# Chunk 0's turned keys and queries earlier on TensorE, one copy moved to ScalarE, and the first late sum of squares and the late root drawn forward

## The chip, the cores and the metric

One core of one Trainium2 chip runs the whole program. The metric is device time in microseconds (us) of one execution; the runs of the kernel before stand under the profile heading.

## The reference

Two transformer-like layers over x of shape (2, 1024, 128), all float32, in one launch:

```
xn = layernorm(x)
x  = x + attn(xn) + moe64(xn)      # layer 0
xn = layernorm(x)
x  = x + rwkv(xn) + moe8(xn)       # layer 1

attn:  h = layernorm(xn)*w + b; q,k,v = h @ qkv_w.T + qkv_b   (16 heads of 8)
       q = q/|q|, k = k/|k|; softmax(q @ k.T * sqrt(8)) @ v; xn + out @ out_w.T + out_b
moe64: top 3 of 64 experts, capacity 64; gelu(xe @ w1 + b1) @ w2 + b2, weighted sum
```

The change lies in the start of `attn`: q and k are divided by their lengths, written as pairs of float16 (a high and a low half), and turned so that the head dimension lies on the partitions.

## The kernel before

The 2048 tokens are 16 tiles of 128, worked in four chunks of 512 tokens (`NC` = 4, `CH` = 4). Chunks 0 and 1 (`EARLY` = 2) are the first sequence of 1024 tokens and are all that the attention needs at first; chunks 2 and 3 are prepared later, between the tiles of the attention.

A program is written by hand for each engine, and each engine runs its own list in the order written; semaphores join the lists. Nothing is scheduled by a planner, so a wait on one engine holds everything that stands behind it there.

The start of the program, chunk by chunk: TensorE turns the normalised rows, multiplies by the q, k and v weights and the gate (`queries_keys`, `value_rows`, `gate_logits`); VectorE adds the bias and stores q and k (`projected`, L724 and L728); ScalarE squares (L487), VectorE sums the squares per head (L715), ScalarE takes the root (L492), VectorE inverts it and scales k (L754 to L758), GpSimd scales q (L362); ScalarE writes the high halves (`high_keys` L497, `high_queries` L502), VectorE and GpSimd the low halves (`low_keys` L764, L367). TensorE then turns the halves with 16 transposes for each of keys and queries of a chunk into PSUM (the tensor `scores`, of four banks: keys in banks 0 and 1, queries in 2 and 3), and VectorE copies 2048 float16 of each partition to `KT` or `QT` (L734). The queries of chunk 1 are turned later, after tile 0 of the attention, into two other banks (`next_queries`, L1307 on TensorE, L748 on VectorE).

For chunks 2 and 3 GpSimd squares q and k (`late_squares`, L357), VectorE sums them (`late_sums`, L770), and ScalarE takes one root for both (L544, it waits for both sums). Directly behind that root ScalarE has the exponential of the decay (L546, which needs another table, loaded by ACT_TABLE_LOAD), and then all the exponentials of the attention (L558).

TensorE's list between the projections and the attention is: four transposes of the layer-1 weights and one of `small_rows` (L1277, L1279), turned keys 0, turned queries 0, turned keys 1 (L1295), and then, after waiting for `kt_sb` 2, `qt_sb` 1 and `lg_sb` 4, the scores. A tile of the attention is 128 keys by 512 queries by 4 heads: TensorE computes scores for two heads at a time (L1334, into `scores`), ScalarE takes the exponential of two banks (L558, two per tile), TensorE multiplies by the values (L1348). There are 128 tiles. Work of the 64-expert layer stands between the tiles at fixed tile numbers: the counts at tile 9, slots and late splits on VectorE at tiles 8 to 18, the inversion at 22, and six tiles for each of eight rounds of four pairs of experts from tile 32 on. The weight loads (L282, L286) are issued by SyncE when `late_split` and `inverted` have come. After the attention comes layer 1 (L1596, L1605, L1080).

VectorE, when keys 0 and 1 and queries 0 are copied, does the top 8 of the gate (L835, L838), the copy of chunk 1's queries (L748), and then the expert masks (L845 to L853).

Of the kernel before, what the change touches and what calls it, by code (L numbers as in the profile page):

```python
# [8 lines left out]
ACT = mybir.ActivationFunctionType  # L9
# [14 lines left out]
def build(nc, x_d, ln_w_d, ln_b_d, qkv_w_d, qkv_b_d, out_w_d, out_b_d, gate_w_d, gate_b_d, w1_d, b1_d, w2_d, b2_d,  # L24
# [4 lines left out]
    CH = 4  # L29
# [56 lines left out]
    with ExitStack() as ctx:  # L86
# [355 lines left out]
        def _(act):  # L442
# [55 lines left out]

            def high_queries(c):
                act.wait_ge(s["qn_ready"], c + 1)  # L500
                src = QKA[:, 0, CH * c:CH * c + CH, :].rearrange("p t (h d) -> p (t h) d", d=HD)
                a.activation(QSs[c][:, :, 0:2, :], src.unsqueeze(2).to_broadcast([P, CH * HEADS, 2, HD]), ACT.Copy).then_inc(s["hi_q"], 1)  # L502
# [39 lines left out]
            high_queries(1)  # L542
            act.wait_ge(s["late_sq"], NC - EARLY)
# [120 lines left out]
        def _(dve):  # L664
# [66 lines left out]
            def split_cols(c, dst, bank, ready, done):  # L731

                dve.wait_ge(s[ready], c + 1)
                v.tensor_copy(dst[:, :, BLK * c:BLK * c + BLK], S[:, bank:bank + 2].rearrange("p b n -> p (b n)").bitcast(F16)  # L734
                              .rearrange("p (g n) -> p g n", g=NHG)).then_inc(s[done], 1)

            def keys_cols(c):
                split_cols(c, KT, 0, "kt_ps", "kt_sb")

            def queries_cols(c):  # L740
                split_cols(c, QT, 2, "qt_ps", "qt_sb")
# [18 lines left out]
            def low_keys(c):  # L760
                dve.wait_ge(s["hi_k"], c + 1)
                k = KSs[c % 2]
                ka = QKA[:, 1, CH * c:CH * c + CH, :].rearrange("p t (h d) -> p (t h) d", d=HD)
                v.tensor_tensor(k[:, :, 1:4:2, :], ka.unsqueeze(2).to_broadcast([P, CH * HEADS, 2, HD]), k[:, :, 0:4:2, :],  # L764
                                ALU.subtract).then_inc(s["lo_k"], 1)

            def late_sums(c):

                dve.wait_ge(s["late_in"], c - EARLY + 1)
                v.tensor_reduce(NL[:, c - EARLY, :], TMPs[c % 2].rearrange("p (n d) -> p n d", d=HD), AX, ALU.add).then_inc(s["late_sq"], 1)  # L770
# [9 lines left out]
            projected(3)  # L780
            keys_cols(0)
            low_keys(1)
            queries_cols(0)
            late_sums(2)
            keys_cols(1)
            late_sums(3)
# [53 lines left out]
            next_queries()  # L840
# [6 lines left out]
            link(last)  # L847
            link(v.tensor_tensor(MH[:], EQ[:, 0], EQ[:, 1], ALU.add))
# [362 lines left out]
        def _(pe):  # L1211
# [60 lines left out]

            pe.wait_ge(s["w1_in"], 16 * 5)
# [7 lines left out]
            pe.wait_ge(s["const_ready"], 3)  # L1281
            pe.wait_ge(s["ht_sb"], NC)
            for c in range(EARLY):

                for src, bank, hi, lo, done, freed in ((KSs[c % 2], 0, "hi_k", "lo_k", "kt_ps", "kt_sb"),
                                                       (QSs[c % 2], 2, "hi_q", "lo_q", "qt_ps", "qt_sb"))[:2 - c]:
                    pe.wait_ge(s[hi], c + 1)
                    pe.wait_ge(s[lo], c + 1)
                    if c:
                        pe.wait_ge(s[freed], c)  # L1290
                    cols = src.rearrange("p (t g j) w d -> p t g (j w d)", t=CH, g=NHG)
                    for g in range(NHG):
                        dst = S[:, bank + g // 2].bitcast(F16).rearrange("p (g t n) -> p g t n", g=2, t=CH)
                        for t in range(CH):
                            last = tr(dst[:, g % 2, t, :], cols[:, t, g, :], ident16[:])  # L1295
                    last.then_inc(s[done], 1)
# [362 lines left out]
```

## Time and profile before

| what | value |
|---|---|
| median of 3 runs | 529.93 us (527.74 to 531.07) |
| the profiled execution: its time / span | 532.37 us / 530.6 us |
| PE (TensorE) busy | 488.2 us, 92% |
| ACT (ScalarE) busy | 373.5 us, 70% |
| DVE (VectorE) busy | 301.7 us, 57% |
| POOL (GpSimd) busy | 145.0 us, 27% |
| mean granted TensorE clock | 0.977 |

PE is TensorE's matmuls, ACT is ScalarE, DVE is VectorE, POOL is GpSimd. Times in the profile count from the start of the span. The busy shares are averages over stages with different limits; the change touches only the stretch from about 36 to 56 us, so what counts is who waits for whom there and what follows from the moment at which the exponentials begin.

### The profile page before, as it was taken

The numbers are of one execution on the slowest core, as the hardware profiler recorded it, in microseconds if no ns is written. First come the engines' busy times: TensorE is split into PE (matmuls) and PEld (weight loads), VectorE is DVE, ScalarE is ACT, GpSimd is POOL, SyncE is SP. The second block draws the span as 40 slices with busy tenths as digits, with TensorE's granted clock in tenths as the row PEclk, the third lists the DMA queues.
The fourth block names the chain that finished last, engine by engine and source line by source line (L and its number), as shares of the span: only waits on it lengthen the run. The fifth ranks groups of instructions, "written<-read, shape, count | busy, mean of one in ns | idle before, by whom it ended". The sixth has DMA issues, their size and how long they took to land.

```text
span 530.6 us, 11403 instructions
## 1 busy us (share of the span) xinstructions
PE 488.2 (92%) x4633; PEld 264.9 (50%) x4634; DVE 301.7 (57%) x791; ACT 373.5 (70%) x463; POOL 145.0 (27%) x133
## 2 busy tenths in 40 slices
PE   2974999999999999999998999999899999999996
PEld 1772323343464465464454232323366767776775
DVE  6689779734333533532521116158846993995895
ACT  3764888876889789878888999889734635543641
POOL 4069000110232032033000255515560647300120
PEclk9996799999999999999998999999999999999999
DMA  5200000193488787887641611100100020000000
GB/s 147 80 2 0 1 2 2 48 305 116 119 236 278 244 250 260 258 262 240 204 142 58 194 33 34 36 7 16 32 16 1 15 51 15 22 1 0 22 0 21
DMA packets 38542, 50.01 MB, mean 94 GB/s; under 512 B 3581, under 2 KB 20250, under 8 KB 38490
## 3 DMA queue, kind: packets, MB, share of 16 engines
q1 hardware_dynamic: 35524, 43.84, 25.5%
q0 software_dynamic: 2560, 5.25, 5.0%
q8 instruction: 37, 0.61, 0.5%
q10 hardware_dynamic: 406, 0.20, 0.1%
q14 instruction: 15, 0.12, 0.1%
HBM read 45.07 MB, written 4.19 MB: 93 GB/s over the span
## 4 chain that ended last, share of the span: by engine, by line
PE 49%; ACT 17%; DVE 6%; issue 5%; DVEq 0%
ACT region_b L558 11%; PE bank L1348 11%; PE bank L1605 9%; PE scores L1596 9%; PE scores L1334 5%; PE bank L1394 4%; PE bank L1382 3%; ACT xn L564 2%; PE bank L1404 2%; PE bank L1465 2%; DVE region_a L1069 2%; ACT L558 2%; ACT L564 2%; DVE base L1080 1%; PE bank L1359 1%
## 5 line engine op out<-in xcount | busy, mean ns | idle before, releaser
L558 ACT ACTIVATE region_b<-scores 128x1024 f32<-128x1024 f32 x256 | 242.4, 1046 | 51.6 <-PE scores L1334 51.4
L1348 PE MATMUL bank<-region_b 128*16 128x256 f32 x2048 | 149.2, 391 | 0.0
L1334 PE MATMUL scores<-region_b 32*128 32x512 f16 x512 | 83.5, 392 | 18.3 <-ACT region_b L558 15.8
L620 ACT ACTIVATE region_b<-scores,small_cols 128x512 f32<-128x512 f32 x64 | 43.5, 685 | 48.6 <-PE scores L1596 48.6
L388 POOL DMA_INDIRECT region_a<-xn_rows,slot_token x32 | 32.5, 1015 | 164.9 <-DVE h_rows L910 108.1
L1348 PEld LDWEIGHTS bank<-region_b 128*16 128x16 f32 x2048 | 42.0, 96 | 57.8 <-issue 42.4
L1605 PEld LDWEIGHTS bank<-region_a,region_b 128*128 128x128 f32 x512 | 62.0, 192 | 15.1 <-issue 15.0
L1334 PEld LDWEIGHTS scores<-region_b 32*128 32x128 f16 x512 | 20.9, 91 | 97.1 <-ACT region_b L558 71.3
L1605 PE MATMUL bank<-region_a,region_b 128*128 128x128 f32 x512 | 62.5, 276 | 0.0
L1596 PE MATMUL scores<-x_rows,region_a 128*128 128x512 f32 x128 | 60.8, 597 | 0.0
L1080 DVE SCALAR_TENSOR_TENSOR base<-bank,g,base 128x128 f32<-128x128 f32 x128 | 36.0, 343 | 25.8 <-PE bank L1605 25.5
L397 POOL DMA_INDIRECT xn<-slot_out,slot_gather x24 | 24.7, 1028 | 66.6 <-DMA slot_out<-slots_io 44.7
L910 DVE COPY h_rows<-bank 128x512 f32<-128x512 f32 x32 | 22.1, 692 | 24.6 <-PE bank L1382 24.6
L926 DVE TENSOR_TENSOR slots_io<-bank,region_a 128x512 f32<-128x512 f32 x8 | 5.5, 692 | 51.6 <-PE bank L1404 51.6
L1382 PE MATMUL bank<-region_a,slots_io 128*64 128x512 f32 x128 | 32.8, 610 | 0.2
L1404 PE MATMUL bank<-region_a,xn 128*64 128x128 f32 x512 | 32.4, 280 | 0.5 <-issue 0.5
L1404 PEld LDWEIGHTS bank<-region_a,xn 128*64 128x64 f32 x512 | 28.4, 139 | 7.8 <-issue 7.8
L1596 PEld LDWEIGHTS scores<-x_rows,region_a 128*128 128x128 f32 x128 | 22.3, 191 | 18.8 <-issue 18.6
L397 POOL DMA_INDIRECT y_rows<-slot_out,slot_gather x24 | 25.4, 1058 | 22.5 <-DMA y_rows<-slot_out,slot_gather 15.2
L817 DVE COPY av_out<-bank 128x512 f32<-128x512 f32 x16 | 11.1, 692 | 34.5 <-PE bank L1348 32.2
L918 DVE TENSOR_TENSOR xn<-bank,region_a 128x512 f32<-128x512 f32 x32 | 21.3, 687 | 15.6 <-PE bank L1394 15.6
L1394 PE MATMUL bank<-ident,h_rows 128*128 128x128 f32 x128 | 21.3, 299 | 0.0
(240 smaller groups left out, 559.8 us busy)
## 6 DMA issues: line engine op xcount, KB each, us to landing
region_a<-in_L_ffn_w SPq DMA_DIRECT2D x64, 512.0 KB, 5.5
region_a<-in_L_ffn_b SPq DMA_DIRECT2D x17, 128.0 KB, 7.0
slot_out<-slots_io SPq DMA_DIRECT2D x8, 256.0 KB, 7.6
region_a<-in_L_attn_x SPq DMA_DIRECT2D x4, 256.0 KB, 4.5
xn_rows<-xn SPq DMA_DIRECT2D x1, 1024.0 KB, 5.1
region_a<-in_L_ffn_W SPq DMA_DIRECT2D x1, 1024.0 KB, 6.3
out<-base SPq DMA_DIRECT2D x4, 256.0 KB, 2.3
region_a<-xn_rows,slot_token POOLq DMA_INDIRECT x32, 3.6
```

The costliest lines, as they stand in the source:

```text
L388: g.indirect_dma_start(ring_in[m % RING], None, xn_rows, bass.IndirectOffsetOnAxis(IDX[:, m:m + 1], 0), bounds_check=T - 1, oob_is_err=Tru ...
L397: g.indirect_dma_start(YGS[c % 2][:, t - CH * c, k, :], None, slot_out, bass.IndirectOffsetOnAxis(SLG[:, k, t:t + 1], 0), bounds_check=SLO ...
L558: a.activation(PR[:, n % PBUF, 2 * h:2 * h + 2, :], S[:, 2 * h:2 * h + 2, :], ACT.Exp, scale=SCALE).then_inc(s["exp_done"], 1)
L620: a.activation(HS[:, e % 2, k], ps[2 * (e % 2) + k][:], ACT.Relu, bias=COL[:, HC1 * e + k:HC1 * e + k + 1]).then_inc(s["relu_done"], 1)
L1080: last = v.scalar_tensor_tensor(y, ps[4 + 3 * (e % 2)][:, D * t:D * t + D], G8[:, c, t, e:e + 1], y, ALU.mult, ALU.add)
L1334: last = mm(S[:, j], KT[head, hg, keys], QT[head, hg, BLK * c:BLK * c + BLK], start=True, stop=True)
L1348: last = mm(AV[32 * j:32 * j + VW, cols], VA[:, tile, HG * (g % NHG) + j, :], PR[:, st % PBUF, j, cols], start=(st == 0 and half == 0), st ...
L1382: last = mm(ps[5 + i % 2][CAP * e:CAP * e + CAP, :], BT[:, P * i + CAP * e:P * i + CAP * e + CAP], ring_w1[i][:, e, :], start=True, stop=True)
L1394: last = tr(ps[5 + i % 2][:, P * c:P * c + P], cols[:, c, :], ident[:])
L1404: last = mm(ps[7][CAP * e:CAP * e + CAP, D * i:D * i + D], HTS[:, i, P * c + CAP * e:P * c + CAP * e + CAP], ring_w2[i][:, e, c, :], start ...
L1596: mm(ps[2 * (e % 2) + k][:], MW1[:, e, P * k:P * k + P], XN2T[:, c, :], start=True, stop=True).then_inc(s["up2"], 1)
L1605: last = mm(ps[4 + 3 * (e % 2)][:, D * t:D * t + D], HS[:, e % 2, k, P * t:P * t + P], MW2[:, e, k, :], start=(k == 0), stop=(k == HC1 - 1))
```

## The change

TensorE turns chunk 0's keys and queries directly behind the last gate logits, ahead of the layer-1 weights. Chunk 0's turned queries are copied by ScalarE (behind the high halves of chunk 1's queries, ahead of the late root) instead of VectorE. VectorE does the first long sum (chunk 2) and chunk 1's low key halves ahead of the copy of chunk 0's turned keys, and the second long sum ahead of the copy of chunk 1's turned keys. VectorE's copy of chunk 1's turned queries moves behind the three expert comparisons. Nothing is added or left out of the arithmetic.

```
 ScalarE
+            def queries_cols():
+                act.wait_ge(s["qt_ps"], 1)
+                a.activation(QT[:, :, 0:BLK], S[:, 2:4]...bitcast(F16)..., ACT.Copy).then_inc(s["qt_sb"], 1)
...
             high_queries(1)
+            queries_cols()
             act.wait_ge(s["late_sq"], NC - EARLY)
             a.activation(NL[:], NL[:], ACT.Sqrt).then_inc(s["late_std"], 1)
 VectorE
             projected(3)
+            late_sums(2)
+            low_keys(1)
             keys_cols(0)
-            low_keys(1)
-            queries_cols(0)
-            late_sums(2)
+            late_sums(3)
             keys_cols(1)
-            late_sums(3)
...
-            next_queries()
             v.tensor_tensor(GE[:], MX[:, :, 0:TOPK], ...)
...
+            next_queries()
             link(v.tensor_tensor(MH[:], EQ[:, 0], EQ[:, 1], ALU.add))
 TensorE
+            pe.wait_ge(s["const_ready"], 3)
+            pe.wait_ge(s["ht_sb"], NC)
+            pe.wait_ge(s["xnt_sb"], NC)
+            pe.wait_ge(s["hi_k"], 1)
+            pe.wait_ge(s["lo_k"], 1)
+            turn_halves(KSs[0], 0, "kt_ps")
+            pe.wait_ge(s["hi_q"], 1)
+            pe.wait_ge(s["lo_q"], 1)
+            turn_halves(QSs[0], 2, "qt_ps")
             pe.wait_ge(s["w1_in"], 16 * 5)
             pe.wait_ge(s["qkv_sb"], 2 * NC)
             pe.wait_ge(s["v_sb"], NC)
             (the layer-1 weights, as before)
-            for c in range(EARLY): (keys 0, queries 0, keys 1)
+            pe.wait_ge(s["hi_k"], 2)
+            pe.wait_ge(s["lo_k"], 2)
+            pe.wait_ge(s["kt_sb"], 1)
+            turn_halves(KSs[1], 0, "kt_ps")
```

VectorE's list from the last gate bias on, as it was (`L734` is the copy of turned keys or queries, `L764` the low key halves, `L770` a long sum, `L748` the copy of chunk 1's queries):

```order
L728 TENSOR_TENSOR region_a<-bank,gate_b 128x256
L734 COPY region_b<-scores 128x4x512
L764 TENSOR_TENSOR region_b<-region_a,region_b 128x128x8
L734 COPY region_b<-scores 128x4x512
L770 TENSOR_REDUCE norms_late<-region_a 128x128
L734 COPY region_b<-scores 128x4x512
L770 TENSOR_REDUCE norms_late<-region_b 128x128
L835 MAX top<-region_a 128x8 x16
L838 MAX_INDEX top_i<-top,region_a 128x8 x16
L748 COPY region_b<-bank 128x2x512 x2
L841 TENSOR_TENSOR gates<-top 128x48
```

The same place in the changed kernel (its lines: `L734` the gate bias, `L739` a copy of turned keys, `L763` the low halves, `L769` a long sum, `L747` the copy of chunk 1's queries):

```order
L734 TENSOR_TENSOR region_a<-bank,gate_b 128x256
L769 TENSOR_REDUCE norms_late<-region_a 128x128
L763 TENSOR_TENSOR region_b<-region_a,region_b 128x128x8
L739 COPY region_b<-scores 128x4x512
L769 TENSOR_REDUCE norms_late<-region_b 128x128
L739 COPY region_b<-scores 128x4x512
L833 MAX top<-region_a 128x8 x16
L836 MAX_INDEX top_i<-top,region_a 128x8 x16
L838 TENSOR_TENSOR gates<-top 128x48
L840 CAST top_if<-top_i 128x48
L842 TENSOR_TENSOR region_a<-iota_e,top_if 128x1024 x3
L747 COPY region_b<-bank 128x2x512 x2
```

One copy is gone from VectorE, both sums stand ahead of the last copy of keys, and chunk 1's queries are copied behind the three comparisons (L842).

TensorE's list between the last projections and the first values, before and after (`scores<-ident,region_a` are the turned halves of chunk 0, `scores<-ident,region_b` those of chunk 1, L1277/L1292 the layer-1 weights):

```order
L1250 MATMUL bank<-gate_w,region_b 128x128 x4
L1277 MATMUL bank<-ident,region_b 128x128 x4
L1279 MATMUL bank<-ident,small_rows 128x18
L1295 MATMUL scores<-ident,region_a 128x128 x32
L1295 MATMUL scores<-ident,region_b 128x128 x16
L1334 MATMUL scores<-region_b 128x512 x10
```

And in the changed kernel:

```order
L1248 MATMUL bank<-gate_w,region_b 128x128 x4
L1276 MATMUL scores<-ident,region_a 128x128 x32
L1292 MATMUL bank<-ident,region_b 128x128 x4
L1294 MATMUL bank<-ident,small_rows 128x18
L1276 MATMUL scores<-ident,region_b 128x128 x16
L1337 MATMUL scores<-region_b 128x512 x10
```

The 32 transposes of chunk 0 now stand ahead of the five of the weights; the order behind them is the same.

## Rows read from the trace of the kernel before

**Rows 1.** Who ScalarE waited for, whole run (us in total, times, longest)
```profile
ACT norms_late L544 <- DVE norms_late L770: 7.8, 1, 7.8
```

**Rows 2.** Timeline of VectorE (start us, us, engine line op, xcount, [idle before])
```profile
38.17 0.41 DVE L728 TENSOR_TENSOR region_a<-bank,gate_b 128x256 f32<-128x256 f32 x1
40.99 1.22 DVE L734 COPY region_b<-scores 128x2048 f16<-128x2048 f16 x1 [2.42 <-PE scores L1295]
42.13 1.77 DVE L764 TENSOR_TENSOR region_b<-region_a,region_b 128x1024 f16<-128x1024 f32 x1
43.83 1.21 DVE L734 COPY region_b<-scores 128x2048 f16<-128x2048 f16 x1
...
46.09 1.21 DVE L734 COPY region_b<-scores 128x2048 f16<-128x2048 f16 x1
47.22 1.21 DVE L770 TENSOR_REDUCE norms_late<-region_b 128x128 f32<-128x1024 f32 x1
...
55.72 1.29 DVE L748 COPY region_b<-bank 128x1024 f16<-128x1024 f16 x2 [2.02 <-PE bank L1307]
...
71.34 0.69 DVE L817 COPY av_out<-bank 128x512 f32<-128x512 f32 x1 [2.64 <-PE bank L1348]
```

**Rows 3.** Timeline of ScalarE, 35 to 60 us
```profile
35.73 0.60 ACT L480 ACTIVATE region_b<-bank 128x512 f32<-128x512 f32 x1 [2.12 <-PE bank L1242]
...
39.57 1.06 ACT L502 ACTIVATE region_b<-region_a 128x1024 f16<-128x1024 f32 x1
48.46 0.42 ACT L544 ACTIVATE norms_late<-norms_late 128x256 f32<-128x256 f32 x1 [7.84 <-DVE norms_late L770]
48.90 1.28 ACT L546 ACT_TABLE_LOAD   x1
...
50.30 4.66 ACT L558 ACTIVATE region_b<-scores 128x1024 f32<-128x1024 f32 x5
56.19 1.94 ACT L558 ACTIVATE region_b<-scores 128x1024 f32<-128x1024 f32 x2 [1.23 <-PE scores L1334]
58.57 1.02 ACT L558 ACTIVATE region_b<-scores 128x1024 f32<-128x1024 f32 x1 [0.45 <-PE scores L1334]
```

**Rows 4.** Timeline of TensorE's matmuls, 35 to 62 us
```profile
35.53 1.06 PE L1250 MATMUL bank<-gate_w,region_b 128*128 128x128 f32 x8
38.34 0.63 PE L1277 MATMUL bank<-ident,region_b 128*128 128x128 f32 x4 [1.76 <-DVE region_a L724]
...
39.07 3.55 PE L1295 MATMUL scores<-ident,region_a 128*128 128x128 f16 x32
44.01 1.05 PE L1295 MATMUL scores<-ident,region_b 128*128 128x128 f16 x16 [1.39 <-issue]
47.36 0.61 PE L1334 MATMUL scores<-region_b 32*128 32x512 f16 x4 [2.30 <-DVE region_b L734]
...
53.72 1.89 PE L1307 MATMUL bank<-ident,region_b 128*128 128x128 f16 x16
...
58.46 1.06 PE L1348 MATMUL bank<-region_b 128*16 128x256 f32 x8
...
60.66 0.63 PE L1348 MATMUL bank<-region_b 128*16 128x256 f32 x8
```

**Rows 5.** Windows of 1 us: busy of PE, PEld, DVE, ACT, POOL, then granted clock, DMA share, GB/s
```profile
39.00:40.00 1.00, 1.00 (x10) 0.97 (x11) 0.00 (x0) 0.99 (x3) 1.00 (x1) 0.52 0.00 0
...
42.00:43.00 1.00, 0.62 (x7) 0.39 (x4) 1.00 (x2) 0.00 (x0) 1.00 (x2) 0.78 0.00 0
...
45.00:46.00 1.00, 0.06 (x2) 0.00 (x0) 1.00 (x2) 0.00 (x0) 1.00 (x2) 0.93 0.00 0
...
59.00:60.00 1.00, 1.00 (x14) 0.24 (x10) 1.00 (x2) 0.70 (x2) 0.00 (x0) 0.74 0.00 0
```

**Rows 6.** Timeline of GpSimd: the squares for the second long sum
```profile
38.32 1.89 POOL L357 TENSOR_TENSOR region_b<-region_a 128x1024 f32<-128x1024 f32 x1 [0.34 <-DVE region_a L724]
```

**Rows 7.** Timeline of SyncE's queue: the first load behind the late splits
```profile
102.23 0.59 SPq L299 DMA_DIRECT2D region_a<-in_L_ffn_b  x1
```

More of the change, by code:

```diff
@@ L497, in high_keys @@
                 a.activation(KSs[c][:, :, 0:4:2, :], src.unsqueeze(2).to_broadcast([P, CH * HEADS, 2, HD]), ACT.Copy).then_inc(s["hi_k"], 1)
+            def queries_cols():
+                act.wait_ge(s["qt_ps"], 1)
+                a.activation(QT[:, :, 0:BLK], S[:, 2:4].rearrange("p b n -> p (b n)").bitcast(F16).rearrange("p (g n) -> p g n", g=NHG),
+                             ACT.Copy).then_inc(s["qt_sb"], 1)
             def high_queries(c):
@@ L729, in projected @@
                                 gate_b[:].unsqueeze(1).to_broadcast([P, CH, E0]), ALU.add).then_inc(s["lg_sb"], 1)
[L731 to L735, printed above, removed]
             def keys_cols(c):
-                split_cols(c, KT, 0, "kt_ps", "kt_sb")
-            def queries_cols(c):
-                split_cols(c, QT, 2, "qt_ps", "qt_sb")
+                dve.wait_ge(s["kt_ps"], c + 1)
+                v.tensor_copy(KT[:, :, BLK * c:BLK * c + BLK], S[:, 0:2].rearrange("p b n -> p (b n)").bitcast(F16)
+                              .rearrange("p (g n) -> p g n", g=NHG)).then_inc(s["kt_sb"], 1)
             def next_queries():
@@ L1271, in _, with turn_halves @@
                     turn_xn(c + 2)
+            def turn_halves(src, bank, done):
+                cols = src.rearrange("p (t g j) w d -> p t g (j w d)", t=CH, g=NHG)
+                for g in range(NHG):
+                    dst = S[:, bank + g // 2].bitcast(F16).rearrange("p (g t n) -> p g t n", g=2, t=CH)
+                    for t in range(CH):
+                        last = tr(dst[:, g % 2, t, :], cols[:, t, g, :], ident16[:])
+                last.then_inc(s[done], 1)
+            pe.wait_ge(s["const_ready"], 3)
[7 more added lines that the diff above has]
+            turn_halves(QSs[0], 2, "qt_ps")
             pe.wait_ge(s["w1_in"], 16 * 5)
@@ L1279, in _ @@
             tr(ps[5][:, 0:18], SMALL[:], ident[0:18, 0:18]).then_inc(s["wt_ps"], 1)
[L1281 to L1296, printed above, removed]
+            pe.wait_ge(s["hi_k"], 2)
+            pe.wait_ge(s["lo_k"], 2)
+            pe.wait_ge(s["kt_sb"], 1)
+            turn_halves(KSs[1], 0, "kt_ps")
             def next_queries():
```

## The prediction

> **What bounds the kernel now.** I read the list of waits by engine first, then the timelines of the four engines from 35 to 60 us, then the granted clock in windows of one microsecond. The longest wait of ScalarE that the change touches is the root of the late norms: it waits 7.8 us for VectorE's second long sum [rows 1]. The timeline shows why this counts. VectorE has nothing to do for 2.42 us until the first turned keys come, then works without a gap: copy, low halves, copy, sum, copy, and last the second sum, which ends at 47.22 + 1.21 = 48.43 [rows 2]. The root starts at 48.46, the table load at 48.90, and the first exponential at 50.30 [rows 3]. From the end of the sum to the first exponential it is thus 1.87 us: root, table load, decay. TensorE had started the first scores at 47.36 [rows 4] and then waited for ScalarE. So the moment at which the attention begins is set by this chain: weights turned (waiting until 38.34), 32 transposes until 42.62, VectorE's queue of six until 48.43, root and table, 50.30.
>
> Behind that moment everything stands in relation to the tiles: VectorE waits for TensorE at tile 8 (2.64 us at 71.34 [rows 2]), and the expert loads are issued at 102.23 [rows 7], right behind a late split in VectorE's list at tile 18. I found nothing between 56 us and the end that waits for an event fixed in time: the loads, the gathers and the last stage all start from something that a tile releases. So a start that comes some microseconds earlier should come through to the end.
>
> **The change, part by part.**
>
> TensorE. The last gate logits end at 35.53 + 1.06 = 36.59 [rows 4]. What the 32 transposes of chunk 0 need is there by then, so they start there instead of at 39.07. Sixteen took 1.05 us at the full clock (44.01) and 3.55 / 2 = 1.78 us in the run of 32 [rows 4], where the granted clock was half (0.52 at 39 us [rows 5]). I take the full clock, since TensorE has been busy until 36.59: 2.1 us, so keys are turned at 37.6 and queries at 38.7. The weights follow, 0.63 and some 0.2 us, done at 39.5. They had ended at 39.1; ScalarE's two copies of them and the high halves of chunk 1 (39.57 to 40.63 [rows 3]) then move back 0.4 us at most.
>
> VectorE. Its bias work ends at 38.58 and it no longer waits the 2.42 us. I take starts from one instruction to the next: a copy 42.13 - 40.99 = 1.14, the low halves 43.83 - 42.13 = 1.70, a sum 47.22 - 46.09 = 1.13 as for a copy (both last 1.21) [rows 2]. Sum 38.55 to 39.68; low halves to 41.38; copy of keys 0 to 42.52 (visible at 42.6); second sum to 43.73 with its end. The squares for it are ready at 38.32 + 1.89 = 40.21 [rows 6], so it does not wait. That is 48.43 - 43.73 = 4.70 us earlier than before.
>
> ScalarE. It takes over the copy of chunk 0's turned queries, of 2048 elements per partition. The trace has no such copy on ScalarE. From 512 elements in 0.60 us and 1024 in 1.02 us, both read from PSUM [rows 3], an element costs (1.02 - 0.60) / 512 = 0.82 ns, and 2048 elements 1.02 + 0.84 = 1.86 us. The lower bound is the 1.21 us of VectorE's copy [rows 2], the upper one twice two exponentials' worth, 2 x 1.94 = 3.9 us. With 1.9 us it runs from 40.7 (or 41.1) to 42.6 (43.0), ahead of the second sum at 43.73. So it costs nothing: it is hidden in what is left of the 7.8 us of waiting. The cover is 0.7 to 1.1 us; at 3.9 us it would cost 1.3 us of the gain. On VectorE the same copy took 1.14 us of a queue that sets the end. The Trainium skill, in "ScalarE: Activation LUTs", Rules for kernel authors, speaks against such a move: plain arithmetic belongs on VectorE, which is faster per element. The duration rows agree with that (1.2 against about 1.9 us), but here it is the queue that counts; by the page's rule alone the copy would lose 0.7 us, by the timeline it removes 1.14 us from the path.
>
> The root now starts at 43.76, and with the same 1.84 us from root to exponential (48.46 to 50.30) ScalarE is ready at 45.6: 4.7 us earlier.
>
> The scores. What is late next is the copy of keys 1. The transposes of chunk 1 need keys 0 copied, at 42.6. TensorE has then been idle since 39.5, about 3.1 us. Rows show what that does: the granted clock fell to half at 39.04 (0.52 in 39 to 40) after a wait of 1.76 us, was full again from 42.4 (0.78 in 42 to 43), and fell at 45.9 after 1.39 us idle, 1.05 us of work and idle again [rows 4, 5]. So after 3.1 us I take the low level of 1.2 GHz for these 16: 1.89 us, as the 16 transposes at 53.72 took it, which ends at 44.5; at 2.4 GHz it would be 1.05 us and 43.7. The copy then ends at 45.75 (or 44.95), and the first scores start 0.06 us later. Two of the four matmuls of 0.61 us and the hand-over are about 0.45 us (an estimate, less than the 0.65 us from 55.54 to 56.19 that four matmuls and the exponential's start need). First exponential: 46.25 at the low level, 45.6 at the full one, where the table is last again. **Gain: 50.30 - 46.25 = 4.05 us, or 4.7 us.** Of the root's 4.7 us the low clock takes 0.65 us back.
>
> What follows. The first tiles ran at half clock before: ScalarE waited 1.23 and 0.45 us for scores at 56.19 and 58.57 [rows 3], and the clock rose only in 59 to 60 (0.74 [rows 5]), 5.8 us after TensorE's first long busy stretch began at 53.72 [rows 4]. The second of these waits goes if the clock rises one or two microseconds sooner after the start of the same stretch; they grow if it rises later. I cannot tell from rows which; the bounds are +1.0 (the 0.45 and half of the 1.23 us gone) and -1.0, and I take +0.3, because the 5.8 us leave more room for a sooner rise than for a later one: at 39.04 the clock fell in the midst of work and was full again 3.4 us later. The Trainium skill, in "TensorE: Matmul & The Clock Gate", The HAM clock gate, says that this watching is free-running and not tied to the kernel's start; by it this term can differ from run to run of the same kernel.
>
> VectorE's second edit. The copy of chunk 1's queries waited 2.02 us for TensorE and took 1.29 us [rows 2]. Now three comparisons fill the wait. It moves the expert masks about 2 us further forward, but they have slack of several microseconds, and before tile 8 VectorE waits 2.64 us for TensorE anyway [rows 2]. Nobody waits for the queries before tile 32. Nothing gained, nothing lost; it only makes sure that the top 8, which start with the copy of keys 1, do not become a new bound.
>
> **Sum.** 4.05 + 0.3 = 4.35 us, rounded 4.4. Against the profiled execution: 532.37 - 4.4 = 528.0 us; it lies 2.4 us above the median, and the three runs spread over 3.3 us, so I set the same gain against the median: 529.93 - 4.4 = 525.5 us.
>
> **The rivals.**
>
> Full clock for chunk 1's keys, and an earlier rise in the first tiles: 4.7 + 1.0 = 5.7 us, 524.2 us. For it: before, the same 16 transposes ran at the full clock, after 1.39 us idle. Against it: 3.1 us idle now.
>
> The gain comes at the start and part is given back: some wait between tile 8 and the last stage that this profile hides behind ScalarE's pace takes over, for example VectorE, which is which has much to do from 71.34 to the loads at 102.23 [rows 2, 7]. If half is lost: 2.2 us, 527.7 us. Against it: VectorE's stretch itself starts from TensorE's tile 8, so it moves along.
>
> ScalarE's copy becomes the bound, at 3.9 us (above): gain 4.4 - 0.7 = 3.7 us at 46.9 for the first exponential, 526.2 us. It lies within the range and close to the forecast.
>
> Slower: the granted clock stays low for longer in the first tiles. At the low level the values of a half tile take 1.06 instead of 0.63 us, and four score matmuls 0.61 us [rows 4], so a half tile (two of them) is an estimated 1.5 us of TensorE, where ScalarE's own pace is 4.66 / 5 = 0.93 us [rows 3]: 0.6 us more. Seven half tiles more at the low level (10 us) take the whole 4.4 us back; beyond that the kernel is slower, with twelve of them by 2.8 us: 532.7 us. For it: the clock stayed low from 45.9 to 59 us. Against it: in the stretch from 53.72 on, whose work is the same now, it did rise after 5.8 us.
>
> That the change doesn't do what it says: if ScalarE waits on something else at the start, such as the weights' transposes, which it waits for ahead of the copy; they end at 39.5, so this would need several microseconds more. Then no gain, 529.9 us.
>
> **How the numbers follow.** Forecast of 4.4 us (with the slow copy taken in): 0.66. Full clock, 5.7 us: 0.14. Half given back: 0.12. No effect: 0.04. Slower: 0.04. A comparison of medians of this kernel can tell about 1%, 5.3 us, from no change. The forecast lies below that by only 0.9 us and the runs scatter by 1.6 us about their median, so a quarter of its chance and most of the full-clock case go to faster: 0.28. Slower by over 1% is 0.04. The range takes in the forecast with its bounds (3.0 to 5.4 us, scatter of about 1.3 us), the 5.7 us case and the half-lost one: 523.2 to 528.5.
>
> **What would show it.** In the changed profile: 32 transposes starting at about 36.6 in about 2.1 us; ScalarE's copy of 2048 elements at 1.9 us, ending before 43.5; the root at 43.8 with a wait of about 1 us instead of 7.84; 16 transposes at 42.6 in 1.9 us; the first exponential at 46.2, and from there the same tiles some 4 us earlier: the first load at about 98 instead of 102.23. The prediction is wrong if the first exponential is 4 us earlier and the end is not, or if the copy on ScalarE takes over 3 us.

## The result, and the profile after

| | before | changed |
|---|---|---|
| median | 527.79 us (22 runs, 527.04 to 533.93) | 525.96 us (22 runs, 523.27 to 530.0) |
| mean of these runs | 528.98 us | 526.08 us |
| profiled execution: time / span | 532.37 / 530.6 us | 525.94 / 524.1 us |
| mean granted TensorE clock, profiled | 0.977 | 0.984 |

The ratio is 0.9947 with a 95% interval of 0.9926 to 0.9968: a gain of 0.5%, 2.8 us (1.7 to 3.9). The interval excludes no change, but the gain is below the 1% that the prediction took as the least that medians can tell. Runs in a disturbed state are left out of the comparisons.

In the changed kernel's trace I read the same timelines as before. ScalarE first (start us, us, engine line op, xcount, and in brackets the idle time before it and who ended it):

```profile
38.77 1.06 ACT L507 ACTIVATE region_b<-region_a 128x1024 f16<-128x1024 f32 x1
39.71 1.88 ACT L501 ACTIVATE region_b<-scores 128x2048 f16<-128x2048 f16 x1
42.79 0.42 ACT L550 ACTIVATE norms_late<-norms_late 128x256 f32<-128x256 f32 x1 [1.20 <-DVE norms_late L769]
43.22 1.28 ACT L552 ACT_TABLE_LOAD   x1
44.52 0.20 ACT L552 ACTIVATE w_decay<-small_cols 128x1 f32<-128x1 f32 x1
45.60 4.69 ACT L564 ACTIVATE region_b<-scores 128x1024 f32<-128x1024 f32 x5 [0.89 <-PE scores L1337]
51.52 1.94 ACT L564 ACTIVATE region_b<-scores 128x1024 f32<-128x1024 f32 x2 [1.23 <-PE scores L1337]
53.91 6.72 ACT L564 ACTIVATE region_b<-scores 128x1024 f32<-128x1024 f32 x7 [0.45 <-PE scores L1337]
```

The wait of 7.84 us ahead of the root [rows 3] is now the copy of 1.88 us and a wait of 1.20. The last thing that the first exponential waits for is no longer the root and its table but the scores (0.89 us). VectorE and TensorE, same columns, show why:

```profile
37.37 0.41 DVE L734 TENSOR_TENSOR region_a<-bank,gate_b 128x256 f32<-128x256 f32 x1
37.70 1.20 DVE L769 TENSOR_REDUCE norms_late<-region_a 128x128 f32<-128x1024 f32 x1
38.83 1.67 DVE L763 TENSOR_TENSOR region_b<-region_a,region_b 128x1024 f16<-128x1024 f32 x1
40.42 1.21 DVE L739 COPY region_b<-scores 128x2048 f16<-128x2048 f16 x1
41.55 1.20 DVE L769 TENSOR_REDUCE norms_late<-region_b 128x128 f32<-128x1024 f32 x1
43.68 1.22 DVE L739 COPY region_b<-scores 128x2048 f16<-128x2048 f16 x1 [0.92 <-PE scores L1276]
```

```profile
35.62 1.95 PE L1276 MATMUL scores<-ident,region_a 128*128 128x128 f16 x32
...
41.77 1.86 PE L1276 MATMUL scores<-ident,region_b 128*128 128x128 f16 x16 [3.44 <-DVE region_b L739]
44.96 0.61 PE L1337 MATMUL scores<-region_b 32*128 32x512 f16 x4 [1.32 <-DVE region_b L739]
```

VectorE no longer waits for turned keys 0 (2.42 us before [rows 2]). TensorE turns chunk 0 in 1.95 us at the full clock, is then idle for 3.44 us, and turns chunk 1 at the low one (the granted clock is 1.00 until 40 us and 0.50 from 41 us on): 1.86 us instead of 1.05 [rows 4].

All times in this trace are 0.80 us early already at the last gate bias (37.37 against 38.17 [rows 2]), ahead of everything that the change touches (more on it at the end). So I measure from the end of the common part: **from the start of the last gate bias to the first exponential it was 50.30 - 38.17 = 12.13 us and is 45.60 - 37.37 = 8.23 us: 3.90 us gained**. From there to the first weight load it was 102.23 - 50.30 = 51.93 us [rows 3, 7] and is 97.36 - 45.60 = 51.76:

```profile
97.36 0.59 SPq L299 DMA_DIRECT2D region_a<-in_L_ffn_b  x1
```

So the gain comes through to there. Of the 6.5 us between the two spans, 0.8 + 3.9 + 0.2 = 4.9 us are made by then. The rest comes late, from a fall of the clock that is in the one trace and not in the other. This is a stretch of the last stage in the changed kernel (busy us of PE, PEld, DVE, ACT, POOL, then granted clock, DMA share, GB/s):

```profile
370.00:395.00 25.00, 23.57 (x194) 13.52 (x193) 16.73 (x54) 12.45 (x16) 13.36 (x11) 1.00 0.09 22
```

and the same stretch of the kernel before:

```profile
370.00:395.00 25.00, 23.58 (x218) 12.02 (x213) 16.58 (x56) 13.73 (x16) 14.63 (x13) 0.93 0.12 28
```

The 0.93 is 3.5 us at half clock, or 1.75 us lost. The 6.5 us of the two spans are therefore not the change's gain; the 2.8 us of the ratio are.

### The profile page after: what moved, and what is told of

The parts are those of the page before. It is cut to its first block, busy times and chain, and to the rows that moved or that the text cites. A ratio compares the mean times of both kernels' runs of the same rounds, so it can differ in the third digit from the quotient of the medians.

```text
span 524.1 us, 11404 instructions
## 1 busy us (share of the span) xinstructions
PE 484.6 (92%) x4634; PEld 262.5 (50%) x4634; DVE 302.1 (58%) x790; ACT 375.5 (72%) x464; POOL 144.7 (28%) x133
## 4 chain that ended last, share of the span: by engine, by line
PE 50%; ACT 17%; DVE 6%; issue 5%; DVEq 0%
ACT region_b L564 11%; PE bank L1351 11%; PE bank L1608 9%; PE scores L1599 9%; PE scores L1337 5%; PE bank L1397 4%; PE bank L1385 3%; ACT xn L570 2%; PE bank L1407 2%; PE bank L1468 2%; DVE region_a L1067 2%; ACT L564 2%; ACT L570 2%; DVE base L1078 1%; PE bank L1362 1%
## 5 line engine op out<-in xcount | busy, mean ns | idle before, releaser
L1351 PE MATMUL bank<-region_b 128*16 128x256 f32 x2048 | 147.4, 387 | 0.0
```

The lines of the kernel that those rows point to most:

```text
L1351: last = mm(AV[32 * j:32 * j + VW, cols], VA[:, tile, HG * (g % NHG) + j, :], PR[:, st % PBUF, j, cols], start=(st == 0 and half == 0), st ...
```

## The experiments

Twelve kernels ran in three sets of four. The first set (queries on VectorE, sums last, TensorE's old order, two stretches filled) ran on another chip, on which the kernel before takes 547.24 us, the others on chips on which it takes 528.2. Of each I give the ratio to the kernel before on its own chip, and, from its trace, the stretch from the start of the last gate bias to the first exponential and from that bias to the first weight load, since these two hold neither the beginning of the run nor later falls of the clock. The front of the kernel took the same on that chip as on the others: 7.26 us to the first exponential in two kernels of the first set and in three of the others. Medians of 6 to 12 runs scatter by about 1 us, so the stretches carry the comparisons, not the totals. Each stretch comes from one trace of its kernel.

| kernel | ratio to before (95%) | bias to first exponential | bias to first load |
|---|---|---|---|
| before | 1 | 12.13 | 64.06 |
| changed | 0.9947 (0.9926 to 0.9968) | 8.23 | 59.99 |
| changed again | 0.9956 (0.9922 to 0.9989) | 8.24 | 59.80 |
| only ScalarE's copy | 0.9977 (0.9949 to 1.0004) | 11.16 | 62.14 |
| only the sums' order | 0.9947 (0.9914 to 0.9981) | 8.39 | 60.08 |
| changed, queries on VectorE | 0.9929 (0.9891 to 0.9966) | 8.39 | 60.26 |
| changed, sums last | 0.9936 (0.9896 to 0.9975) | 8.58 | 60.51 |
| changed, TensorE's old order | 0.9935 (0.9899 to 0.9970) | 7.26 | 58.24 |
| changed, next queries back | 0.9925 (0.9891 to 0.9960) | 8.24 | 59.86 |
| changed, two stretches filled | 0.9872 (0.9819 to 0.9925) | 7.26 | 59.28 |
| changed, all filled | 0.9915 (0.9884 to 0.9946) | 7.26 | 58.27 |
| before, all filled | 0.9974 (0.9948 to 0.9999) | 12.12 | 61.84 |
| all filled, copy late | 0.9886 (0.9843 to 0.9930) | 7.26 | 57.39 |
| the same, TensorE's old order | 0.9895 (0.9848 to 0.9942) | 7.26 | 57.41 |

**Chunk 0's queries back on VectorE.**

```
 VectorE:  late_sums(2); low_keys(1); keys_cols(0)
+          queries_cols()            # S[:, 2:4] to QT, was on ScalarE
           late_sums(3); keys_cols(1)
```

> The changed kernel with the copy of chunk 0's turned queries given back to VectorE, behind the copy of keys 0; all else as changed. Theory (VectorE's queue and the low clock of the 16 transposes set the first exponential): the second long sum ends 1.13 us later, the root chain is then the last to arrive and the copy of keys 1 also stands behind it; first exponential 0.3 to 1.1 us later than in the changed kernel's trace (45.60), the whole 0.1 to 0.2% longer than changed. Rival (VectorE's copy was covered, the gain is all from the sums' place): no difference in the first exponential.

Measured: 0.16 us later (8.39), below the 0.3 to 1.1 that was expected. The two sides are now level: VectorE's copy of keys 1 had been waiting 0.92 us for TensorE's slow transposes, so the additional copy fills that wait; the root chain is 1.1 us later and just becomes the last one again. Beside the sums' new place and the low clock the move to ScalarE is worth 0.16 us. At the full clock it is worth more, as the experiment with only the sums' order shows.

**The sums in their old place.**

```
 VectorE:
-          late_sums(2); low_keys(1); keys_cols(0); late_sums(3); keys_cols(1)
+          keys_cols(0); low_keys(1); late_sums(2); keys_cols(1); late_sums(3)
```

> The changed kernel with VectorE's long sums in their old place (keys 0, low keys 1, sum, keys 1, sum last). Theory: the root waits for the last sum again, VectorE's five instructions end at about 45.3 instead of the second sum's 42.75 in the changed trace, so root, table and decay end at about 46.9: first exponential 1.0 to 1.5 us later than 45.60. The whole 0.2 to 0.3% longer than changed. Rival (the order of the sums does not count once TensorE's turns are early): within 0.3 us of 45.60.

Measured: 0.35 us later, neither the 1.0 to 1.5 us of the theory nor quite the rival. The root did wait for the last sum, but it came earlier than I had reckoned, because the low halves are done one sum sooner and the transposes of chunk 1 ran at the full clock (TensorE of this kernel):

```profile
41.27 1.09 PE L1276 MATMUL scores<-ident,region_b 128*128 128x128 f16 x16 [2.26 <-DVE region_b L763]
```

With the turns early, the sums' place is worth 0.35 us between these two traces. That is a difference of two things: with the 16 transposes at the full clock the new place comes to 7.26 us (the filled kernel below), 1.32 us less than here, and the low clock of the changed kernel takes 0.97 us of it back.

**TensorE's old order.**

```
 TensorE:
-          turn keys 0, turn queries 0
           layer-1 weights, small rows
+          turn keys 0, turn queries 0
           turn keys 1
```

> The changed kernel with TensorE's old order (layer-1 weights first, then keys 0, queries 0, keys 1), VectorE and ScalarE as changed. Theory: keys 0 are turned at 40 to 41, before VectorE wants them at 41.4 after the first sum and the low halves, so nothing is lost there; ScalarE's copy of the queries comes 1 to 3 us later but before the root or at most 1 us behind; and TensorE is busy until about 42, so that chunk 1's 16 transposes may run at full clock. First exponential from 0.7 us earlier to 0.7 us later than changed: TensorE's early turns are worth nothing. Rival (the early turns carry the gain): 2 us or more later than changed, since that is the time by which the keys are turned earlier.

Measured: 0.97 us *earlier* than changed (0.7 us was the most expected). TensorE and ScalarE of this kernel:

```profile
38.63 1.96 PE L1276 MATMUL scores<-ident,region_a 128*128 128x128 f16 x32
42.14 1.05 PE L1276 MATMUL scores<-ident,region_b 128*128 128x128 f16 x16 [1.55 <-DVE region_b L739]
```

```profile
40.62 1.88 ACT L501 ACTIVATE region_b<-scores 128x2048 f16<-128x2048 f16 x1 [0.44 <-PE scores L1276]
43.15 0.42 ACT L550 ACTIVATE norms_late<-norms_late 128x256 f32<-128x256 f32 x1 [0.65 <-DVE norms_late L769]
...
44.99 4.66 ACT L564 ACTIVATE region_b<-scores 128x1024 f32<-128x1024 f32 x5
```

The keys are turned 2.7 us later and still before VectorE asks for them. TensorE's work lies nearer to chunk 1's turns, its idle stretch is 1.55 instead of 3.44 us, and the 16 transposes took 1.05 us. The root is the last to come again, with no wait for scores. That the early turns bring nothing is shown by VectorE's second sum, which starts 4.18 us behind the gate bias in both. What they cost is the clock. In the four traces with 3.44 us of idle time ahead of the 16 transposes (changed, changed again, next queries back, queries on VectorE) these took 1.86 us; in the ten others, with 0.67 to 2.98 us of idle time there, 1.05 to 1.09 us. Where the clock stands could differ in other executions of the same kernels; each but the changed one was traced once.

**Two idle stretches filled.**

```
 TensorE:
+          for j in range(20): transpose(ps[6][:, 0:P], WL1[:, 0], ident)    # read by nobody
           turn keys 1
+          for j in range(8):  transpose(ps[6][:, 0:P], WL1[:, 0], ident)
```

> The changed kernel with 20 float32 transposes of a weight tile into a free bank in TensorE's idle stretch ahead of chunk 1's keys, and 8 more behind them; their results are read by nobody. Theory (the fall of the granted clock in that idle stretch costs the transposes 0.8 us and keeps the first tiles at the low level): the 16 transposes take 1.05 instead of 1.86 us, first exponential 0.5 to 0.8 us earlier relative to the copy of keys 0, ScalarE's waits of 1.23 and 0.45 us behind it shrink by up to 1.5 us together; the whole 0.2 to 0.4% shorter than changed. Rival (the low level costs nothing that counts, or the extra transposes delay the turned keys): same or up to 0.5 us longer.

Measured: 0.97 us earlier, and the transposes of chunk 1 took 1.05 us. The waits behind (1.24, 0.45, 0.38 us) stayed, against the theory: TensorE was idle for 1.14 and 0.61 us among the first scores and the clock fell there (granted 1.00 until 46 us, 0.50 from 47 us on). The ratio of 0.9872 is from five runs with a wide interval; 0.2 to 0.4% below the changed kernel was expected, and the 0.7 us that this kernel is ahead at the first load (59.28 against 59.99) do not explain so low a total. What does is open.

**All filled.** As above with 22 and 9, and 8 and 3 more such transposes between the first scores.

> As the filled experiment (idle stretches of TensorE ahead of and behind chunk 1's keys filled with float32 transposes nobody reads, 22 and 9), and 8 and 3 more between the first scores. Theory: with no idle stretch left the granted clock stays at 2.4 GHz through the first tiles in every execution, the waits of ScalarE of 1.24, 0.45 and 0.38 us shrink to under 0.9 us together: 1 to 1.5 us shorter than the kernel with two stretches filled, 0.987 to 0.984 of before. Rival (the clock falls anyway, or the fillers delay scores): no gain on the kernel with two stretches filled.

Measured: 58.27 us to the first load, 1.0 us sooner than with two stretches filled (59.28). The ratio is 0.9915 and not the 0.984 to 0.987 of the theory, and not below the 0.9872 of the kernel with two stretches filled; the two ran on different chips and their intervals overlap. ScalarE of this kernel:

```profile
43.99 13.00 ACT L564 ACTIVATE region_b<-scores 128x1024 f32<-128x1024 f32 x14
...
68.05 14.77 ACT L564 ACTIVATE region_b<-scores 128x1024 f32<-128x1024 f32 x16 [2.70 <-PE scores L1341]
```

The waits of the first tiles are gone: fourteen exponentials without a gap. But at tile 8 ScalarE waits 2.70 instead of 1.41 us. VectorE and TensorE of this kernel at that place:

```profile
62.56 1.75 DVE L789 RECIPROCAL norms_late<-norms_late 128x256 f32<-128x256 f32 x1
64.35 0.69 DVE L815 COPY av_out<-bank 128x512 f32<-128x512 f32 x1
```

```profile
65.18 1.06 PE L1355 MATMUL bank<-region_b 128*16 128x256 f32 x16 [1.22 <-DVE av_out L815]
```

VectorE had waited 2.64 us ahead of this copy in the kernel before [rows 2]. Now it has no wait, its queue is the bound, and TensorE waits for it. By the end of the 23rd exponential the fillers have brought 2.8 us (28.63 us behind the gate bias against 31.43 in the repetition of the changed kernel); 1.3 of them go in the longer wait at tile 8, and 1.5 are left at the first load (58.27 against 59.80).

**The kernel before, filled.** 10 such transposes ahead of the layer-1 weights, 10 ahead of chunk 1's keys, 17 behind, 26 and 3 between the first scores.

> The kernel before with its idle stretches of TensorE filled in the same manner (10 transposes ahead of the layer-1 weights, 10 ahead of chunk 1's keys, 17 behind them, 26 and 3 between the first scores). Theory: the first exponential comes no earlier (it waits for VectorE's sums, the root and the table: 12.1 us from the gate bias, or up to 0.9 less since the 32 transposes go faster), but the waits behind it shrink: 0.4 to 0.6% shorter than before. The difference between this one and the all-filled changed one is then the change's own gain without the clock: 4.0 to 4.7 us. Rival (the clock is no part of it): same as before.

Measured: the first exponential where it was (12.12 us), the first load 2.2 us sooner, the whole 0.26% shorter (0.01 to 0.52%), less than the 0.4 to 0.6% expected. That the first exponential comes no sooner has a reason of its own. TensorE turned chunk 0's keys at the full clock here (the 32 transposes took 1.96 us instead of 3.55), and VectorE waited for them only 1.58 us instead of 2.42. But the low halves behind them took 2.60 us instead of 1.77, beside GpSimd's own low halves, and ended 5.73 us behind the gate bias in both kernels:

```profile
39.63 1.22 DVE L734 COPY region_b<-scores 128x2048 f16<-128x2048 f16 x1 [1.58 <-PE scores L1300]
40.77 2.60 DVE L764 TENSOR_TENSOR region_b<-region_a,region_b 128x1024 f16<-128x1024 f32 x1
```

```profile
40.16 2.13 POOL L367 TENSOR_TENSOR region_b<-region_a,region_b 128x1024 f16<-128x1024 f32 x1 [0.47 <-ACT region_b L502]
```

This kernel and the all-filled changed one have no fall of the clock in this stretch (granted 1.00 from 36 us to the first load). Between them lie 61.84 - 58.27 = 3.6 us at the first load and 527.44 - 524.02 = 3.4 us in the median. This is the change's gain with the early clock taken out of it, somewhat less than the 4.0 to 4.7 us expected: at tile 8 the all-filled changed kernel waits 1.3 us longer than this one (2.70 against 1.41).

**VectorE's copy late.**

```
 VectorE, from the all-filled changed kernel:
-          next_queries()            # behind the three comparisons
           at tile 8: evacuate(0)
+          next_queries()
           late_split(2, 1)
```

> The all-filled changed kernel, and VectorE's copy of chunk 1's queries moved on, behind the copy of the first values' output at tile 8. Theory: in the all-filled kernel VectorE's own queue had become the bound at tile 8 (no wait ahead of its copy at 64.35, TensorE waited 1.22 us for it, ScalarE 2.70 instead of 1.41). With 1.2 us taken out of that queue ScalarE's wait at tile 8 goes back to about 1.5 us and the first weight load comes 1.0 to 1.3 us earlier relative to the last gate bias (95.00 - 36.73 = 58.27 in the all-filled one, 59.80 in the changed one). Rival (that wait is something else, such as the clock or the masks): 58.27 stays.

Measured: 57.39, that is 0.88 us sooner, somewhat less than 1.0 to 1.3. ScalarE of this kernel at tile 8:

```profile
67.20 14.78 ACT L564 ACTIVATE region_b<-scores 128x1024 f32<-128x1024 f32 x16 [1.50 <-PE scores L1341]
```

1.50 us, as it was to be if VectorE's queue was the cause. Against the kernel before, filled, the first load is now 61.84 - 57.39 = 4.45 us sooner. The median, 523.76 us (0.9886), is the lowest of the four kernels on its chip.

**The same with TensorE's old order** (8 and 9 fillers, then as above):

> The same, with TensorE's old order (layer-1 weights, 8 fillers behind the turns of chunk 0, 9 behind those of chunk 1). Theory: TensorE's early turns are worth nothing, so the first exponential comes as with the early turns and all filled, 7.26 us behind the gate bias, and the whole takes the same as its sister to within 0.1%. Rival (early turns matter once the clock is full): 0.5 us or more later.

Measured: the same two stretches to within 0.02 us. Its median is 524.81 us, 1.05 us above its sister in six runs each, with overlapping intervals, so the totals do not settle the 0.1%; by the median alone the rival (0.5 us or more) would be right, by both stretches the theory.

**The next queries back.**

```
 VectorE:
+          next_queries()            # ahead of the gates' difference
...
-          next_queries()            # behind the three comparisons
```

> The changed kernel with VectorE's copy of chunk 1's queries back ahead of the gates' difference. Theory: VectorE waits 1 to 2 us for TensorE's turn of those queries again, the masks end about 2 us later, nobody waits for them; first exponential and first weight load unchanged relative to each other (51.8 us apart), whole within 0.1% of changed. Rival (the masks or the top 8 set the pace at tile 9): the load comes 1 us or more later.

Measured: nothing at the load (59.86 against 59.80), as expected. The median is 524.24 us against 526.18 of the changed kernel beside it, where 0.1% was expected, with overlapping intervals. VectorE does not lose by it, it gains slack: it waits only 0.74 us for the turned queries, and ahead of tile 8's copy 2.28 us, against 1.34 and 1.15 us in the two traces of the changed kernel. The masks end 1.1 us earlier, not 2 us later. The reason stands under what I had not expected.

**Only ScalarE's copy**, the rest as before:

```
 ScalarE:  high_queries(1)
+          queries_cols()
 VectorE:  keys_cols(0); low_keys(1)
-          queries_cols(0)
           late_sums(2); keys_cols(1); late_sums(3)
```

> The kernel before with one part of the change: ScalarE copies chunk 0's turned queries, VectorE does not. Theory: VectorE's queue behind the turned keys is one copy of 1.13 us shorter and the last sum, root and table come that much earlier: first exponential 11.0 us behind the gate bias instead of 12.13; the whole 0.2% shorter than before. Rival (only the parts together help): same as before.

Measured: 11.16 us, a gain of 0.97 of the expected 1.13. The rest went into VectorE's copy of chunk 1's keys, which now starts 0.14 us late because TensorE's 16 transposes end only at 44.86.

**Only the sums' order**, both copies on VectorE, TensorE as before:

```
 VectorE:
-          keys_cols(0); low_keys(1); queries_cols(0); late_sums(2); keys_cols(1); late_sums(3)
+          late_sums(2); low_keys(1); keys_cols(0); queries_cols(0); late_sums(3); keys_cols(1)
```

> The kernel before with another part alone: VectorE's order is sum, low keys 1, keys 0, queries 0, sum, keys 1 (both copies stay on VectorE, TensorE in its old order). Theory: the first sum and the low halves fill the 2.42 us in which VectorE waited for turned keys, and the root no longer waits for the last copy: second sum ends 3.5 us earlier, first exponential 8.6 us behind the gate bias instead of 12.13; the whole 0.5% shorter than before. So this part alone carries most of the gain. Rival (the early turns and ScalarE's copy carry it): at most 1.5 us earlier.

Measured: 8.39 us, even 0.2 better than reckoned, and 0.9947 as the whole change. VectorE of this kernel:

```profile
38.00 1.20 DVE L770 TENSOR_REDUCE norms_late<-region_a 128x128 f32<-128x1024 f32 x1
39.12 1.67 DVE L764 TENSOR_TENSOR region_b<-region_a,region_b 128x1024 f16<-128x1024 f32 x1
40.72 2.34 DVE L734 COPY region_b<-scores 128x2048 f16<-128x2048 f16 x2
42.99 1.20 DVE L770 TENSOR_REDUCE norms_late<-region_b 128x128 f32<-128x1024 f32 x1
44.12 1.21 DVE L734 COPY region_b<-scores 128x2048 f16<-128x2048 f16 x1
```

It stands without a gap from the gate bias on. So 3.74 of the 3.90 us come from the reordering on VectorE alone: 2.4 us are the filled wait, 1.1 us the copy that no longer stands ahead of the last sum, 0.2 us shorter steps. Early turns and ScalarE's copy together add 0.16 us.

But this 0.16 us is what is left of two larger effects. With the sums in their new place, four of the kernels give all cases (bias to first exponential; the traces are from several chips):

| | TensorE's old order | early turns |
|---|---|---|
| queries copied by VectorE | 8.39 (only the sums' order) | 8.39 (queries on VectorE) |
| queries copied by ScalarE | 7.26 (TensorE's old order) | 8.23 (changed) |

In the old order of TensorE ScalarE's copy brings 1.13 us, a whole copy of VectorE. The early turns bring nothing beside VectorE's copy and cost 0.97 us beside ScalarE's. That the clock is this cost is shown by the kernel with two stretches filled, where the early turns stay and 7.26 us come back. So two parts of the change, without the early turns, have the first exponential 4.87 us sooner than before, and all of it together 3.90.

**The changed kernel again:**

> The changed kernel itself, once more, beside the experiments. Theory: the gain of the start (12.13 us from the last gate bias to the first exponential before, 8.23 changed) comes again to within 0.8 us, depending on which of the 16 transposes run at the low clock; ratio to before 0.992 to 0.995. Rival (what the first trace showed at the start was partly luck of its execution): the stretch differs by more than 1 us from 8.23.

Measured: 8.24 us, and the same 1.86 us for chunk 1's transposes; the ratio, 0.9956, lies just outside the 0.992 to 0.995. The stretch repeats to 0.01 us, while its span is 521.7 us against 524.1. In the 2.4 us between two executions of one kernel are 0.64 us at the beginning (36.73 against 37.37 at the gate bias), 0.2 us from there to the first load, and some 1.55 us at the end of the expert rounds: from the first weight load to the last write of slots it took 284.99 - 96.53 = 188.46 us here and 287.37 - 97.36 = 190.01 there, where the granted clock was 0.79 from 280 to 288 us and is 1.00 here.

## Why the prediction was right

**The bound and the mechanism.** Right: the root and its table set the start, behind VectorE's sums. The second sum went from an end at 48.43 to 42.75; less the 0.80 us of the beginning that is 4.88 us, against 4.70 predicted.

**The weak point.** The first exponential was forecast at 46.25, on the clock of the trace before, with scores as the last to come and the 16 transposes at the low level. Measured is 45.60, or 46.40 on that clock. The gain at this point was 4.05 forecast, 3.90 measured. The 16 transposes took 1.86 us (1.89 forecast). The 0.15 us lie in the step from the first scores to the exponential, estimated at 0.45 us against the row of 0.65 us, and measured at 45.60 - 44.96 = 0.64. That the low clock takes away part of what the root gains is shown by the filled kernel: 0.97 us come back when TensorE's idle stretch there is filled (0.65 us forecast).

**ScalarE's copy.** 1.88 us measured, 1.86 forecast, with 1.20 us of wait left behind it. It costs nothing. That "by the timeline it removes 1.14 us from the path" holds for it alone (0.97) and beside the sums' order (1.13); once the early turns stand beside it, it is 0.16.

**TensorE's early turns.** I counted them as the step that frees VectorE. They are not: VectorE does the sum and the low halves first and asks for keys only 2.7 us later. With the old order the first exponential was 0.97 us sooner. The prediction had the cost ("Of the root's 4.7 us the low clock takes 0.65 us back") but not its cause: it is the early turns that move TensorE's work away from chunk 1's transposes and leave 3.44 us of idle time instead of 1.55. My text had all numbers for that (keys turned by 37.6, wanted at 41.4) and did not draw the conclusion.

**What follows behind.** The +0.3 us for a sooner rise of the clock were 0.17 us (51.93 to 51.76), and 0.37 us in the repetition (51.56). The waits of 1.23 and 0.45 us were the same; the third one of 0.29 us went.

**VectorE's second edit.** "Nothing gained, nothing lost" holds for the time. That it had slack was right; that it moves the masks forward was wrong: they end later than with the copy in its old place. The slack at tile 8 shrank from 2.64 to 1.34 us, and a start faster by more than that would have met it, as the all-filled kernel did.

**The size.** 4.4 us forecast against the median, 2.8 us (1.7 to 3.9) by the ratio, 1.8 us between the medians, 2.9 us between the means; 525.96 us stands where 525.5 was said, and that it lies so close is luck: the median of the kernel before is 527.79 us over 22 runs and not 529.93 as over the first three, and the gain was smaller than said by nearly as much. The step that was mis-sized is the sum's last one, which set the gain of one trace against the median of three runs. The traces show 4.1 us up to the first load (64.06 - 59.99; 4.3 against the repetition), and the shortest runs 527.04 - 523.27 = 3.8 us. What is lacking to 2.8 us was not traced. It may come from where the later falls of the clock lie in each execution: 13 of the 22 runs of before are within 1 us of its shortest, but only 4 of the 22 of the changed one, whose largest group is near 525.9. Its profiled run is one of that group, and the fall at 280 to 288 us is what it has more than its repetition. Whether the changed kernel gets into such executions more often is not settled: the falls lie in stretches that both kernels have alike, and I have no trace of before in one of its short runs. In the second set of runs it was 15 of 34 runs of before and 4 of 12 of the changed kernel, a smaller difference, so chance is possible.

## What to carry to other kernels

Ask for every wait on an in-order engine which work that is ready stands behind it; two ready instructions moved ahead of one wait, and a third ahead of a copy, gave 3.74 us, where the change of three engines gave 3.90. Before moving work forward on an engine, compare the moment at which its result is there with the moment at which it is wanted: the turned keys had been early enough already. Try the parts of a change in pairs too: a small sum of two parts (0.16 us) can be a gain of 1.13 and a loss of 0.97. And look at the duration of the first matmuls behind an idle stretch of TensorE that a change makes longer: here they took 1.86 us instead of 1.05.

## What I had not expected

**The granted clock is not told at the start of the trace.** Eight matmuls of the same form at 20 us took, in the kernel before and in the changed one:

```profile
20.28 1.87 PE L1242 MATMUL bank<-w_cols,region_b 128*128 128x128 f32 x8
```

```profile
20.29 1.06 PE L1240 MATMUL bank<-w_cols,region_b 128*128 128x128 f32 x8
```

The clock column reads 1.00 for both. The durations are those of the two levels, so in the one execution the clock rose after these eight and in the other before them. This is the 0.80 us by which the changed trace was ahead at the gate bias: it belongs to the execution and not to the kernel. The Trainium skill, in "TensorE: Matmul & The Clock Gate", The HAM clock gate, says that the chip's watching runs free of the kernel's start, and the traces agree with it: the same kernel twice had the gate bias at 37.37 and at 36.73.

**VectorE is slowed by GpSimd's additions.** In the changed kernel two operations on 48 elements, which take 0.20 and 0.18 us elsewhere, and GpSimd beside them:

```profile
50.34 0.90 DVE L838 TENSOR_TENSOR gates<-top 128x48 f32<-128x48 f32 x1
51.16 1.29 DVE L840 CAST top_if<-top_i 128x48 f32<-128x48 uint32 x1
```

```profile
47.45 4.95 POOL L379 TENSOR_TENSOR base<-base,out_b 128x512 f32<-128x512 f32 x4
```

The cast ends at 52.45, GpSimd's last addition at 52.40; the subtraction ends at 51.24, where the last addition starts at 51.1. With the copy of chunk 1's queries back ahead of them, the two come later and took 0.22 and 0.17 us. That saves more than the 0.74 us of waiting ahead of that copy, and is why the masks end 1.1 us earlier there. The all-filled kernel meets the same: its three comparisons took 4.51 us instead of 3.50 beside GpSimd's last addition, and VectorE was through with this queue only 0.17 us sooner than in the changed kernel (27.58 against 27.75 us behind the gate bias). The Trainium skill, in "GPSIMD Engine Reference", Specifications, says that GpSimd shares its SBUF interfaces with VectorE, with contention where a VectorE instruction reads two inputs from SBUF or runs in a two-port mode. The rows of the subtraction, which reads two, agree in kind; in which mode the cast runs no trace shows. No run changed GpSimd's work, so the cause is read from these coincidences and not tested.

**The other chip.** There the kernel before takes 547.24 us. In the trace of the kernel with the queries on VectorE, a round of the experts there took 21.5 us (from one write of slots to the next, 175.37 to 196.87), where the same round of the kernel before took 19.8 us on its own chip (175.34 to 195.14). These are two kernels, but they differ only in the front. I have not looked for the cause.
